# Key and value convolutions as scaled copies and shifted adds; sums opened by a transpose; a new walk

## The reference

```
y = x @ W                       # 128 features -> 128 channels
z[t, c] = sum over s = 0..3 of w[c, s] * y[t - s, c]    # y is 0 before the first token
out = z * sigmoid(z)
```

## Time and profile before

| | us |
|---|---|
| median of the runs (3) | 1204.84 (1203.2 to 1209.31) |
| profiled execution | 1203.81 |
| its span | 1202.0 |
| TensorE busy | 1103.1 |
| VectorE busy | 895.9 |
| ScalarE busy | 560.2 |
| GpSimd busy | 278.6 |
| mean granted clock of TensorE | 0.925 |

### The profile page before, as it was taken

How to read it: one execution, slowest core, us unless ns; L and a number is a source line. 1 busy time by engine, 2 the same in 40 slices (tenths; PEclk the granted TensorE clock), 3 DMA queues, 4 the chain that set the end, 5 groups by cost and what they waited for, 6 DMA issues and landing times.

```text
span 1202.0 us, 22464 instructions
## 1 busy us (share of the span) xinstructions
PE 1103.1 (92%) x8212; PEld 760.6 (63%) x8212; DVE 895.9 (75%) x3410; ACT 560.2 (47%) x1283; POOL 278.6 (23%) x303
## 2 busy tenths in 40 slices
PE   5888898899799999999999878999979999999997
PEld 3776555464456766777878645463635686677765
DVE  3879899853778767967868799994488866787673
ACT  2267443343222246566557763453424223566753
POOL 1222114334310112311212221335331002322101
PEclk9799799999877899999999888999988679999999
DMA  9000000012322100001111000011223210000000
GB/s 341 9 1 1 1 1 14 22 29 55 82 56 46 27 11 10 10 1 36 36 37 36 1 1 1 1 36 44 54 60 65 45 20 10 18 10 1 1 19 18
DMA packets 80670, 38.06 MB, mean 32 GB/s; under 512 B 65840, under 2 KB 74416, under 8 KB 80304
## 3 DMA queue, kind: packets, MB, share of 16 engines
q1 hardware_dynamic: 80560, 36.63, 12.0%
HBM read 22.03 MB, written 6.29 MB: 24 GB/s over the span
## 4 chain that ended last, share of the span: by engine, by line
PE 57%; DVE 28%; ACT 5%; issue 3%; DMA 2%; POOL 2%; SPq 1%; DVEq 0%; ACTq 0%; POOLq 0%
PE psum L831 5%; PE psum L935 5%; PE psum L443 5%; DVE pool L1482 4%; DVE sol_t L1479 4%; PE psum L761 3%; PE psum L927 3%; PE psum L448 3%; PE psum L698 2%; PE psum L800 2%; DVE small L1012 2%; PE psum L787 2%; PE psum L921 2%; PE psum L923 2%; ACT pool L1727 2%
## 5 line engine op out<-in xcount | busy, mean ns | idle before, releaser
L2039 POOL TENSOR_TENSOR small<-small,minus_half 128x4 f32<-128x4 f32 x88 | 90.8, 1032 | 482.1 <-DVE small L1020 481.9
L1713 ACT ACTIVATE pool<-psum 128x512 f32<-128x512 f32 x160 | 93.5, 597 | 160.5 <-PE psum L761 61.0
L1727 ACT ACTIVATE pool<-pool,small 128x128 f32<-128x128 f32 x256 | 105.2, 484 | 95.3 <-POOL small L2041 95.1
L443 PE MATMUL psum<-sb_const,pool 128*128 128x128 f32 x672 | 108.2, 299 | 15.7 <-ACT pool L1727 6.6
L443 PEld LDWEIGHTS psum<-sb_const,pool 128*128 128x128 f32 x672 | 85.7, 154 | 50.0 <-issue 23.9
L761 PE MATMUL psum<-pool,firw 128*32 128x512 f32 (+7 forms) x960 | 104.4, 591 | 6.2 <-issue 4.4
L831 PE MATMUL psum<-pool,sb_l1a 128*128 128x512 f32 x192 | 88.2, 613 | 0.0
L935 PEld LDWEIGHTS psum<-sb_l1f,pool 128*128 128x128 f32 x640 | 77.8, 192 | 13.6 <-issue 13.1
L935 PE MATMUL psum<-sb_l1f,pool 128*128 128x128 f32 x640 | 80.7, 276 | 0.0
L761 PEld LDWEIGHTS psum<-pool,firw 128*32 128x32 f32 x960 | 33.1, 114 | 68.6 <-issue 68.3
L1482 DVE TENSOR_TENSOR pool<-pool,sol_t 128x126 f32<-128x126 f32 (+22 forms) x248 | 67.0, 270 | 8.5
(11 more groups left out here) (403 smaller groups left out, 2397.5 us busy)
## 6 DMA issues: line engine op xcount, KB each, us to landing
pool<-in_cF SPq DMA_DIRECT2D x16, 256.0 KB, 3.2
pool<-scratch_kk SPq DMA_DIRECT2D x16, 256.0 KB, 4.0
pool<-in_xF SPq DMA_DIRECT2D x8, 256.0 KB, 3.4
pool<-in_x SPq DMA_DIRECT2D x8, 256.0 KB, 4.3
pool<-pool SPq DMA_DIRECT2D x32, 64.0 KB, 2.0
scratch_kk<-pool SPq DMA_DIRECT2D x32, 64.0 KB, 1.9
scratch_xt<-pool SPq DMA_DIRECT2D x16, 128.0 KB, 2.6
pool<-scratch_xt SPq DMA_DIRECT2D x32, 64.0 KB, 2.2
```

Of the source, the lines that this page charges most:

```text
L443: m = e.transpose(f.ap[:, part(b)], src[:, part(b)], ident)
L1713: e.activation(slot(g, i), f.ap, ACT.Copy).then_inc(f.emptied, 1)
L1727: m = e.activation(dst[:, part(b)], src[:, part(b)], ACT.Identity, bias=v["nm"][:, b:b + 1], scale=v["r"][:, b:b + 1])
L2039: e.tensor_tensor(r, r, half[:, 0:GB], ALU.pow).then_inc(*mark("inverse_std", n_var[step, 0, g]))
```

## The change

- **k and v.** TensorE does one product each with Wk and Wv (`wqkv` in place of `wconv` and `wq`). ScalarE copies it four times, each scaled by one tap, to four slots (`tapped`); GpSimd adds three of them, shifted, into the first (`summed`). Then `b_ks` and `b_vs`, new steps of the walk, take tanh on ScalarE and the multiplication on VectorE, now from SBUF. Semaphores `k_made` and `v_made` stand where the bank's release stood.
- **q** goes the same way: four scaled copies, three adds; GpSimd's three multiplications go.
- **Preparation.** Columns of taps come from eight one-column products of TensorE (`s_b1`), in place of the folded weights.
- **Waits.** SP's `b_sh` also waits for the last add of k (slots 8 to 10 are used by it), ScalarE's `b_vT` for the last add of q (slot 2).
- **Sums.** In `a_out`, `c_pv` and `g_b4` the added tile comes first, as a transpose that opens the sum (`opened`); the products follow.
- **The walk** is another order of the same steps, with `b_ks` and `b_vs`.

The walk around the first solve (`b_x.0/0`), before and after:

```diff
-b_ag/0 b_sol/0 b_k/2 f_d.2/3 b_q/2 b_vT/1 b_gg/1 b_k2/2 f_d.3-5/3 f_out/3 f_na/3 b_qs/2 b_fir.0-3/1 b_tr/3 b_qn/1
-b_v/2 b_sh/2 b_kk/1 b_q2/2 b_x.0-7/0 b_ss/2 b_ag/1 b_sol/1 b_q/3 b_x.8-22/0 b_k/3 b_qn/2 b_x.23-30/0 b_xo/0 b_qs/3
+f_e.1/3 b_q2/1 f_e.2-4/3 b_gg/0 b_gg/1 b_v/2 b_q/2 f_e.5/3 b_k/2 b_kk/0 b_ag/0 b_sol/0 f_d.0/3 b_vs/2 b_qs/2 b_sh/2
+f_d.1-3/3 b_ks/2 b_k2/2 b_fir.0-2/1 b_qn/1 f_d.4-5/3 f_out/3 f_na/3 b_x.0-1/0 b_fir.3/1 b_vT/2 b_tr/3 b_kk/1 b_ag/1
+b_sol/1 b_x.2/0 b_k/3 b_q2/2 b_fir.0/2 b_x.3-11/0 b_q/3 b_x.12-30/0 b_xo/0 b_x.0/1 b_v/3 b_qs/3 b_x.1-2/1 b_ss/2
+b_ks/3 b_k2/3 b_fir.1-2/2 b_vs/3 b_sh/3 b_qn/2 b_q2/3 b_fir.3/2 b_x.3-5/1 b_gg/2 b_x.6/1 b_u.0/0 b_x.7/1 b_kk/2 b_ag/2
+b_x.8-9/1 b_sol/2 b_x.10-11/1 b_qn/3 b_p.0/0 b_x.12-18/1 b_vT/3 b_ss/3 b_u.1/0 b_x.19-26/1 b_fir.0-3/3 b_x.27-30/1
```

```diff
         def b_sh(g, k):
...
-            f = fill("b_v", g)
-            o.wait_ge(f.emptied, f.n)
+            o.wait_ge(sem("v_made"), g + 1)
+            o.wait_ge(sem("k_conv"), 3 * g + 3)
...
+        def opened(f, src, b, start):
+
+            e.matmul(f.ap[:, part(b)], src[:, part(b)], ident, start=start, stop=False, is_transpose=True)
...
+        def s_b1(g, k):
+            landed(o, "const", "once_rows")
+            f = begin("s_b1", g, "taps")
+            for i, n in enumerate(("k", "v")):
+                for s in range(4):
+                    m = e.matmul(f.ap[:, 4 * i + s:4 * i + s + 1], wt("once_rows", n + "_conv", s * P, P), ident[:, 0:1],
+                                 start=True, stop=True)
+            m.then_inc(f.filled, 1)
...
             for b in range(GB):
-                e.matmul(f.ap[:, part(b)], slot(g, 3)[:, part(b)], wt("l0a", "w2T"), start=True, stop=False)
-                m = e.matmul(f.ap[:, part(b)], slot(g, 2)[:, part(b)], ident, start=False, stop=True)
+                opened(f, slot(g, 2), b, True)
+                m = e.matmul(f.ap[:, part(b)], slot(g, 3)[:, part(b)], wt("l0a", "w2T"), start=False, stop=True)
...
-        def conv(f, g, i):
-            for s in range(4):
-                m = e.matmul(b4(f.ap)[:, :, s:], wconv[:, i, s, :], b4(slot(g, 1))[:, :, 0:P - s], start=s == 0, stop=s == 3)
-            m.then_inc(f.filled, 1)
...
         def b_k(g, k):
...
-            conv(begin("b_k", g), g, 0)
+            f = begin("b_k", g)
+            e.matmul(f.ap, wqkv[:, part(1)], slot(g, 1), start=True, stop=True).then_inc(f.filled, 1)
...
         def b_kk(g, k):
-            got("b_k", g)
+            o.wait_ge(sem("k_made"), g + 1)
...
-        def b_k(g, k):
-            f = fill("b_k", g)
+        def b_ks(g, k):
             o.wait_ge(sem("k_tanh"), g + 1)
-            e.scalar_tensor_tensor(out=slot(g, 7), in0=slot(g, 14), scalar=1.0, in1=f.ap, op0=ALU.add,
-                                   op1=ALU.mult).then_inc(f.emptied, 1)
+            e.scalar_tensor_tensor(out=slot(g, 7), in0=slot(g, 14), scalar=1.0, in1=slot(g, 7), op0=ALU.add,
+                                   op1=ALU.mult).then_inc(sem("k_made"), 1)
...
+        def tapped(step, g, i, tiles):
+
+            o.wait_ge(made, MADE["s_b1"])
+            f = full(step, g)
+            for s, tile in enumerate(tiles):
+                m = e.activation(slot(g, tile), f.ap, ACT.Copy, scale=taps[:, i, s:s + 1])
+            m.then_inc(f.emptied, 1)
...
         def b_k(g, k):
-            f = full("b_k", g)
-            e.activation(slot(g, 14), f.ap, ACT.Tanh).then_inc(sem("k_tanh"), 1)
+            tapped("b_k", g, 1, (7, 8, 9, 10))
...
+        def b_ks(g, k):
+            o.wait_ge(sem("k_conv"), 3 * g + 3)
+            e.activation(slot(g, 14), slot(g, 7), ACT.Tanh).then_inc(sem("k_tanh"), 1)
...
         def b_vT(g, k):
+            o.wait_ge(sem("q_conv"), 3 * g + 3)
             evacuate("b_vT", g, 2)
...
+        def summed(step, g, done, y, tiles):
+
+            f = fill(step, g)
+            o.wait_ge(f.emptied, f.n)
+            for s, tile in enumerate(tiles, 1):
+                settle()
+                e.tensor_tensor(b4(slot(g, y))[:, :, s:], b4(slot(g, y))[:, :, s:], b4(slot(g, tile))[:, :, 0:P - s],
+                                ALU.add).then_inc(*mark(done, 3 * g + s))
+
         def b_q(g, k):
-            raw, t, y = slot(g, 12), slot(g, 13), slot(g, 15)
-            f = fill("b_q", g)
-            o.wait_ge(f.emptied, f.n)
-            for s in range(1, 4):
-                settle()
-                e.tensor_scalar(t, raw, qtaps[:, s:s + 1], None, ALU.mult).then_inc(*mark("q_tap", 3 * g + s))
-                settle()
-                e.tensor_tensor(b4(y)[:, :, s:], b4(y)[:, :, s:], b4(t)[:, :, 0:P - s], ALU.add).then_inc(
-                    *mark("q_conv", 3 * g + s))
+            summed("b_q", g, "q_conv", 15, (2, 12, 13))
+
+        def b_k(g, k):
+            summed("b_k", g, "k_conv", 7, (8, 9, 10))
```

More of the change, by code:

```diff
@@ L42 @@
[L42 to L51, removed]
@@ L87 @@
-f_d.1-2/6 c_nb/7 f_out/5 f_d.3/6 f_tr/7 f_d.4-5/6 f_out/6 f_lg/7 f_na/5 f_hid.0-1/7 f_na/6 f_hid.2/7 b_q2/4 b_tr/5
-f_mu/7 b_tr/6 f_hid.3/7 b_q/5 b_q/6 b_qn/4 b_k/5 f_cnt/7 f_gl/7 f_hid.4/7 b_qs/5 b_q2/5 b_v/5 b_v/6 b_sh/5 b_k2/5
-b_k/6 b_sh/6 b_vT/5 b_fir.0-3/4 b_qs/6 f_gw/7 b_fir.0-1/5 b_gg/4 b_fir.2/5 f_e.0-4/7 b_vT/6 f_hid.5/7 b_kk/4 b_ag/4
-f_e.5/7 b_ss/5 b_gg/5 f_d.0-3/7 b_qn/5 b_k2/6 b_sol/4 f_d.4/7 b_ss/6 f_d.5/7 f_out/7 f_na/7 b_gg/6 b_q2/6 b_fir.3/5
-b_tr/7 b_kk/5 b_ag/5 b_q/7 b_sol/5 b_x.0-19/4 b_v/7 b_x.20-30/4 b_xo/4 b_qs/7 b_k/7 b_sh/7 b_qn/6 b_x.0/5 b_fir.0-2/6
@@ L92 @@
-b_k2/7 b_fir.3/6 b_x.1-2/5 b_u.0/4 b_kk/6 b_q2/7 b_x.3-12/5 b_p.0/4 b_ag/6 b_vT/7 b_x.13-15/5 b_ss/7 b_u.1/4
-b_x.16-25/5 b_gg/7 b_fir.0-1/7 b_x.26-29/5 b_p.1/4 b_qn/7 b_fir.2-3/7 b_u.2/4 b_sol/6 b_x.30/5 b_xo/5 b_kk/7 b_x.0/6
-b_ag/7 b_sol/7 b_u.0/5 b_x.1-23/6 b_p.2/4 b_at/4 b_u.3/4 b_p.0/5 b_x.24/6 b_us/4 b_x.25-30/6 b_xo/6 b_u.1/5 b_p.1/5
-b_o/4 b_x.0-4/7 b_u.2/5 b_oT/4 b_p.2/5 b_x.5-12/7 b_oF/4 b_u.3/5 b_u.0/6 b_r.0-1/4 b_x.13-30/7 b_xo/7 b_p.0/6 b_at/5
-b_u.1/6 b_lg/4 b_p.1/6 b_us/5 b_u.0/7 b_w/4 b_u.2/6 b_p.0/7 b_o/5 b_p.2/6 b_at/6 b_u.1/7 b_u.3/6 b_us/6 b_oT/5 b_p.1/7
@@ new lines @@
+f_hid.2/1 f_out/0 f_na/0 c_sc/3 f_cnt/1 c_ft/2 f_hid.3/1 f_gl/1 f_hid.4/1 b_tr/0 c_ex/3 b_v/0 c_fa/2 f_hid.5/1 b_k/0
+b_vs/0 b_sh/0 c_pT/3 f_gw/1 c_nb/2 c_pv/3 f_e.0-4/1 f_tr/2 b_q/0 c_na/3 f_lg/2 f_d.0-1/1 f_hid.0/2 c_hF/3 f_e.5/1
+b_qs/0 c_w1/3 f_d.2-4/1 b_ks/0 c_ft/3 b_q2/0 b_k2/0 f_d.5/1 f_mu/2 c_fa/3 b_vT/0 b_fir.0-1/0 f_out/1 f_hid.1-3/2
+c_nb/3 b_ss/0 f_na/1 b_fir.2/0 f_tr/3 f_cnt/2 b_tr/1 f_lg/3 f_mu/3 f_hid.0/3 f_gl/2 f_hid.4/2 b_v/1 b_qn/0 b_fir.3/0
+f_gw/2 f_cnt/3 f_hid.1-2/3 f_e.0-1/2 f_gl/3 b_k/1 f_hid.3/3 b_q/1 f_e.2-3/2 b_ks/1 f_d.0-1/2 f_gw/3 b_k2/1 f_e.4/2
@@ new lines @@
+f_na/4 f_hid.3-4/5 f_tr/6 c_hF/7 f_gw/5 b_tr/4 f_lg/6 f_mu/6 b_k/4 f_hid.0-1/6 f_e.0/5 b_v/4 f_hid.2/6 b_ks/4 b_k2/4
+f_e.1-3/5 b_vs/4 b_sh/4 c_w1/7 f_hid.5/5 f_e.4-5/5 f_cnt/6 f_gl/6 f_d.0-1/5 c_ft/7 f_d.2/5 b_q/4 f_d.3/5 f_hid.3/6
+b_ss/4 f_d.4-5/5 f_gw/6 f_e.0-3/6 c_fa/7 b_qs/4 b_vT/4 f_d.0/6 b_fir.0/4 f_hid.4/6 f_e.4/6 f_hid.5/6 f_e.5/6 f_out/5
+f_d.1-2/6 b_q2/4 c_nb/7 f_d.3/6 f_tr/7 f_d.4/6 f_na/5 f_d.5/6 f_out/6 f_na/6 f_hid.0-1/7 b_tr/5 f_hid.2-3/7 b_tr/6
+b_v/5 f_lg/7 b_gg/4 b_k/5 b_q/5 b_q/6 f_mu/7 b_k/6 f_hid.4/7 b_qs/5 b_vs/5 b_sh/5 b_v/6 b_fir.1/4 b_q2/5 b_fir.2-3/4
@@ new lines @@
+b_ks/5 f_cnt/7 b_k2/5 f_hid.5/7 b_qn/4 b_ks/6 b_vT/5 b_qs/6 b_ss/5 f_gl/7 b_kk/4 b_ag/4 b_gg/5 b_fir.0-1/5 f_gw/7
+b_sol/4 b_vs/6 b_sh/6 b_qn/5 b_fir.2/5 f_e.0/7 b_k2/6 f_e.1-5/7 f_d.0-5/7 b_x.0-1/4 b_q2/6 f_out/7 f_na/7 b_fir.3/5
+b_tr/7 b_kk/5 b_ag/5 b_x.2/4 b_v/7 b_q/7 b_x.3-7/4 b_k/7 b_sol/5 b_vT/6 b_x.8-30/4 b_xo/4 b_x.0-1/5 b_ss/6 b_qs/7
+b_fir.0-2/6 b_x.2-4/5 b_vs/7 b_sh/7 b_qn/6 b_ks/7 b_k2/7 b_fir.3/6 b_x.5-8/5 b_u.0/4 b_gg/6 b_vT/7 b_kk/6 b_ag/6
+b_p.0/4 b_x.9-10/5 b_sol/6 b_ss/7 b_u.1/4 b_x.11-30/5 b_xo/5 b_q2/7 b_x.0/6 b_gg/7 b_fir.0-3/7 b_qn/7 b_x.1-4/6 b_kk/7
@@ L726, in b_v @@
             got("b_tr", g)
-            conv(begin("b_v", g), g, 1)
+            f = begin("b_v", g)
+            e.matmul(f.ap, wqkv[:, part(2)], slot(g, 1), start=True, stop=True).then_inc(f.filled, 1)
         def b_ss(g, k):
@@ L740, in b_vT @@
         def b_vT(g, k):
-            got("b_v", g)
+            o.wait_ge(sem("v_made"), g + 1)
             turn(begin("b_vT", g), slot(g, 5))
@@ L965, in g_b4 @@
             for b in range(GB):
-                e.matmul(f.ap[:, part(b)], slot(g, 10)[:, part(b)], ident, start=b == 0, stop=False)
+                opened(f, slot(g, 10), b, b == 0)
             for i in range(2):
```

165 lines of the change are left out of this document (83 added, 82 removed), and 1 row of the table BANKS.

## The result

The changed kernel takes 1212.9 us (median of 12 runs, 1209.0 to 1217.0); the kernel before took 1204.5 us beside it (12 runs, 1199.0 to 1213.3). The ratio is 1.0064, with a 95% interval of 1.0041 to 1.0087: slower by about 8 us (0.6%), where 1162 and a range of 1145 to 1186 were forecast. The profiled execution took 1212.8 us, its span is 1211.1 us.

What follows compares the result with a forecast made beforehand. TensorE was taken as the main limit, shared with other engines in some stages. 43.8 - 5.5 + 3.6 + 6.5 - 2.6 - 3.7 = 42.1 us off 1203.8 gave 1162 us, range 1145 to 1186 for 8 in 10.

Steps and rivals of the forecast that it cites:

- GpSimd's clash: VectorE's solve steps stretched beside GpSimd's operations: 0.45 us per us, 17.2 us more GpSimd time, charged 2.6 us.
- Only a third on the path: About a third of the added GpSimd time falls where VectorE is on the path: 2.6 of 7.7 us.
- Rival 2: Solves keep their length, the lead is lost; only twelve convolutions ahead of the first solves pay: 1182 us, chance 0.16.
- Convolutions off TensorE: k and v: 96 fewer TensorE records gain 43.8 us, less 5.5 for convolutions during the solve chain's stall.
- Identity products: In `a_out`, `c_pv`, `g_b4`, transposes save one record in two: 3.6 us for `g_b4`, 6.5 for the others.
- Latency: Each k and v is made 3.7 us later behind its product; 3.7 us charged in all, bounds 0 and 59.
- ScalarE, nothing: Scaled copies of q, k, v add 58 us over eight groups, covered by ScalarE's idle time: priced at nothing.
- The walk, nothing: Reordering the steps, with `b_fir.3/1` moved behind the first solve, given nothing by itself; bound +-12 us.
- near 268: Sign: the first solve begins near 268 rather than 293; above 1180 us even so, the lead was lost.
- both signs: Wrong if TensorE's convolution-stage idle time passed 20 us a half, or its clock fell in the first 200 us.
- the third: TensorE waits for longer k and v chains in 200 to 293 and 766 to 867: 1214 us, chance 0.06.
- The fourth chance: No change in time, the gain eaten by a lower clock; chance 0.05.

Runs made afterwards that it cites:

- the kernel with one tap: Kernel before, three of four taps of k and v left out, nothing added elsewhere, old walk: 1193.3 us, ratio 0.9927.
- the pair without clash: Powers replace GpSimd's 72 adds in the changed kernel (1176.6 us), and q's six GpSimd operations a group in the kernel before (1184.7 us).

## Why the prediction was wrong

1. *GpSimd's clash, 2.6 us (bounds 0 and 7.7).* This step failed. It measured 36 us in the change and 18 in the kernel before, so 18 more (20 by the ratios), where 2.6 more was forecast. Set against the 8 to 12 us that the rest of the change gains, it turns the sign; against the 48.4 us that was forecast for TensorE it would not have (see 2). Three things were wrong in it.
   - The rate was a mean over two kinds of operation. In the timeline the stretched steps beside q's multiplies are 0.66, 0.75 and 0.74 us, beside its adds 1.23, 1.06 and 1.03. Less 0.29 an undisturbed step, a multiply costs 0.43 us and an add 0.82. I took 3.7 us over 8.3 us of both, then charged by added GpSimd *time*. But the change adds 48 adds (39 us at 0.82) and takes 24 multiplies away (10 us): 29 us if each had a step of VectorE to stretch, nearly four times the bound of 7.7. Over the whole trace the rows of VectorE that overlap GpSimd's operations are stretched, against others of their shape, by 24.5 us before and 47.9 after: 23 us more, close to that.
   - "Only a third on the path" was a guess from VectorE's share. Most of it was paid: 43.7 us of VectorE's busy time (917.0 less 873.3) cost 36 us in the change, and 21.8 us (895.9 less 874.1) cost 15 to 18 in the kernel before. The clash falls on rows of dependent steps (the solve, the router), where VectorE has nothing else to do and TensorE waits behind.
   - Where the adds would stand was not looked at. I counted stretched steps "some eight a half", and with nine that was nearly right for the solves. But they are nine beside the adds of the half's last group alone, each at the price of an add, and these groups carry 17 to 20 of the 36 us; the other half of the cost, beside the router of the experts and other small steps, I had not looked for.
   An add stretches a solve step, with its two inputs from SBUF, to about its own length: 1.23 us beside an add of 1.29, 1.06 beside 1.11, 1.03 beside 1.07. A multiply does not: beside one of 1.56 us a step takes 0.74 or 0.75. I charged by GpSimd's time and missed that the price goes by the count of stretched steps. Rival 2's 7.7 us, the expectations and some labels put this clash down to a port. No run shows one; what the runs show is the longer steps, 0.43 and 0.82 us each, and the 36 and 18 us of time.
2. *Convolutions off TensorE, 43.8 - 5.5.* The count of records was right and their time nearly (39.6 us less on the lines, where 43.8 was forecast). Their worth was not: 9 to 10 us by the kernel with one tap, and 8 to 12 for the whole change once the clash is out of both. Of the 50 us that left TensorE's lines the pair without clash shows where much of it went. Between the kernel before and the change, both with powers in place of GpSimd's work, TensorE's busy time falls by 25 us (1098.7 to 1073.7) and the time outside it rises by 27 (79.7 to 106.8). The clock is 0.928 and 0.906: 2 x (0.094 x 1180.5 - 0.072 x 1178.4) = 52 us more at the lower level, 26 us of work. So in these two executions about half went into a slower clock and half into waiting. The split isn't firm: the first is faster than its kernel's median and the second slower, and by the mean clocks of six runs each (0.926 and 0.912) it is 32 us at the lower level, 16 us of work. This is the larger error, about 35 us of the 51.
   The step that failed is "every us of TensorE work taken out there is a us of time". It was read from 432 to 640, where TensorE never idles, and nothing was taken out there but `g_b4`. In 200 to 293 TensorE was busy 86.5 of 93 us, and I took that too for its stage. What the work is worth also hangs on the walk. On the new walk 10.7 us of it cost 10 (the identity products put back), and from the old steps on that walk (1236.0 us) to the change without clash (1176.6) it is 59 us, less what q's clash costs there, which wasn't measured. The 8 to 12 us are the difference between two sets of steps, each on the walk made for it.
3. *Identity products, 3.6 + 6.5.* Alone, on the old walk, 0 (1.0015); within the change, 10 us. The size that I forecast, 10.1, is met on the one walk and missed on the other, so it can't be called right. Whether transposes lower the clock more than other work is open: its mean is 0.916 with transposes and 0.920 with plain products of the same length, in two kernels whose times can't be told apart.
4. *Latency, 3.7 (bounds 0 and 59).* GpSimd's part of it is about 0: 67 us less on GpSimd changed nothing. *ScalarE, nothing:* its busy time is 608.9 us (forecast 618), and the kernel without clash has all of it and still takes 1176.6. That it costs nothing, in throughput or in the chains, was not measured by itself.
5. *The walk, nothing (bound 12).* The first solve begins at 274.9, 18 us earlier than before, and at 268.6 without the clash; "near 268" was nearly right, and so was that this shows a lead. In the kernels without clash the lead is lost within each half: the last step of the solves starts at 384.6 and 384.7 us in the first and at 943.2 in both in the second, though the first solve began 16.4 us apart (285.0 and 268.6). With the clash it is worse than lost: in the second half that step starts at 973.9 us, at 964.4 before, and these 9.5 us are about what the change costs. That is the second rival's mechanism, "the lead is lost". I gave it 0.16 and 1182 us; without the clash the kernel takes 1176.6. A walk is worth up to 40 us here, so pricing a new one at nothing, with a bound of 12, said too much: the old walk was fitted to the old steps, and the gain of any edit read off it includes that fit.
6. *What would show it wrong:* both signs that I named came, in other places. TensorE's time outside work in 200 to 293 is 8 us, not 20 (over the span it is 133 us, where no more than 115 was forecast); the clock in the first 200 us is 0.91, as before. But from 293 to 432 the clock fell from 0.83 to 0.77, and from 766 to 867 TensorE's busy time fell from 97.8 to 89.0 us of 101, at a clock of 0.89, 0.98 before. The signs were bound to stages, while what is removed in one stage was lost in the next.

Of the rivals, the third (slower, 1214) came nearest in time and was wrong in mechanism. The fourth chance, 0.05, was for no change in time, the gain eaten by a lower clock. The clock did fall, from 0.925 to 0.904 in the profiled executions, and by the estimate under 2 it took about half of the 50 us or less. A rival with the clash at 0.82 us an add is missing from the list; it would have been the slower end.

Open: whether the lower clock or the waiting comes first. No experiment here sets the clock by itself. Nor does less work alone explain it: the old steps on the new walk, with the same work, have a mean clock of 0.909, lower than the 0.911 of the kernel with one tap, so the walk may have its part in what the clock lost in the change. No walk was fitted anew to the kernel with q on TensorE, which could move it either way.
